# Message layers of a GNN kernel: rows in DRAM in node order, far table stored by blocks, one-byte destination lists

## The reference, cut to what matters

```python
def message_part(x, edge_index, ...):           # two layers
    h = x @ W_enc.T + b_enc
    row, col = edge_index
    for l in range(2):
        m = jnp.concatenate([h[row], h[col]], axis=-1)
        m = jax.nn.relu(m @ msg_W1[l].T + msg_b1[l])
        m = m @ msg_W2[l].T + msg_b2[l]
        agg = jax.ops.segment_sum(m, col, num_segments=N)
        upd = jnp.concatenate([h, agg], axis=-1) @ upd_W[l].T + upd_b[l]
        h = layer_norm(h + upd, ln_g[l], ln_b[l])
    return h @ W_out.T + b_out

def linear_part(x, edge_index, ...):            # three layers
    for i in range(3):
        agg = segment_sum(h[src], dst) / max(degree, 1)
        h = agg @ Wl[i].T + bl[i] + h @ Wr[i].T  # relu between layers
```

## Time and profile before

| | us |
|---|---|
| median of 3 runs | 3507.04 (3503.56 to 3512.03) |
| the profiled execution, its own time | 3502.89 |
| its span in the profile | 3501.0 |
| PE / DVE / ACT / POOL busy | 2972.4 / 2400.5 / 2058.7 / 800.4 |
| granted TensorE clock, mean | 0.931 of full speed |

### The profile page before, as it was taken

The page is one execution under the profiler, slowest core; times in us unless marked ns, Lnnn a source line. Parts: engine busy times, 40 slices in busy tenths (PEclk is TensorE's granted clock), DMA queues, the critical chain, the costliest instruction groups (busy, mean ns, idle before and its releaser), DMA issues.

```text
span 3501.0 us, 221482 instructions
## 1 busy us (share of the span) xinstructions
PE 2972.4 (85%) x88750; PEld 2729.9 (78%) x88750; DVE 2400.5 (69%) x5707; ACT 2058.7 (59%) x3873; POOL 800.4 (23%) x1161
## 2 busy tenths in 40 slices
PE   3665666699989998799989997789999799999998
PEld 2544544588878887688878887688888799999998
DVE  6899998555545556666645555699999865556555
ACT  1333333577766666777756665667777555555555
POOL 1222215200012225400012124334333411111111
PEclk7777777899999999999999999799999999999999
DMA  3000002699978883599977875055555478877888
GB/s 68 9 7 7 6 6 53 141 214 216 216 180 201 198 201 88 121 219 217 223 180 195 199 197 123 16 164 172 170 170 171 137 219 276 274 243 232 263 269 251
DMA packets 423266, 570.13 MB, mean 163 GB/s; under 512 B 129597, under 2 KB 277877, under 8 KB 423186
## 3 DMA queue, kind: packets, MB, share of 16 engines
q1 hardware_dynamic: 390475, 541.83, 57.2%
q0 software_dynamic: 8000, 16.40, 4.7%
q10 hardware_dynamic: 24710, 10.93, 1.2%
HBM read 459.97 MB, written 108.98 MB: 163 GB/s over the span
## 4 chain that ended last, share of the span: by engine, by line
PE 57%; DVE 16%; issue 9%; DMA 9%; SPq 3%; POOL 2%; ACT 2%; DVEq 1%; POOLq 0%; ACTq 0%
PE psum L1544 16%; PE psum L1315 15%; PE psum L1333 7%; PE psum L1319 7%; DMA tabf<-slots_turned 5%; DVE arena L1583 5%; PE psum L1531 4%; PE psum L1511 2%; PE psum L684 1%; PE psum L1519 1%; POOL arena L2019 1%; DVE Hf L1057 1%; DVE Hf L918 1%; DVE AGGf L963 1%; POOL tabf L2002 1%
## 5 line engine op out<-in xcount | busy, mean ns | idle before, releaser
L1315 PE MATMUL psum<-tabf,arena 125*32 125x128 f16 x40256 | 1112.4, 220 | 105.9 <-issue 58.4
L1315 PEld LDWEIGHTS psum<-tabf,arena 125*32 125x32 f16 x40256 | 949.5, 97 | 197.8 <-issue 129.9
L1319 PE MATMUL psum<-arena 96*32 96x128 f16 x20928 | 1054.3, 221 | 10.4 <-issue 10.4
L1366 ACT ACTIVATE arena<-psum 128x512 f32<-128x512 f32 x1300 | 770.5, 596 | 426.1 <-PE psum L1319 387.7
L1319 PEld LDWEIGHTS psum<-arena 96*32 96x32 f16 x20928 | 693.6, 95 | 19.0 <-issue 9.6
L1544 PE MATMUL psum<-tabr,cellr 125*125 125x256 f32 x5000 | 620.2, 284 | 14.4 <-ACT cellr L1462 14.4
L1544 PEld LDWEIGHTS psum<-tabr,cellr 125*125 125x125 f32 x5000 | 602.8, 187 | 15.8 <-issue 15.8
L1333 PE MATMUL psum<-arena 128*32 128x129 f32 x10400 | 564.1, 278 | 1.7 <-issue 1.7
L1462 ACT CAST cellr<-arena 125x630 fp32r<-125x630 f16 x500 | 359.9, 720 | 270.2 <-PE psum L1544 197.0
L1573 ACT CAST arena<-psum 125x500 f16<-125x500 f32 x625 | 358.9, 578 | 153.0 <-PE psum L1511 109.6
L1401 DVE TENSOR_TENSOR AGGf<-AGGf,psum 125x129 f32 x404 | 116.0, 287 | 435.6 <-PE psum L1333 432.9
(11 more groups left out here) (302 smaller groups left out, 4369.1 us busy)
## 6 DMA issues: line engine op xcount, KB each, us to landing
arena<-cells_kept SPq DMA_DIRECT2D x500, 315.0 KB
cells_kept<-arena SPq DMA_DIRECT2D x625, 126.0 KB
arena<-slots_turned SPq DMA_DIRECT2D x152, 384.0 KB
tabf<-slots_turned SPq DMA_DIRECT2D x150, 384.0 KB
arena<-slots_turned SPq DMA_DIRECT2D x152, 192.0 KB
tabf<-slots_turned SPq DMA_DIRECT2D x150, 192.0 KB
arena<-slots_turned SPq DMA_DIRECT2D x50, 512.0 KB
tabf<-slots_turned SPq DMA_DIRECT2D x50, 512.0 KB
```

The costliest lines, as they stand in the source:

```text
L1315: pe.matmul(psCell[b][q:q + GW, g * D:(g + 1) * D], fr, rows, start=g == 0 and p == 0, stop=False, tile_position=(0, q), skip_group_check= ...
L1319: m = pe.matmul(psCell[b][q:q + GW, g * D:(g + 1) * D], toB[part][:, here + q:here + q + GW], cur[:, part, g, :], start=g == 0 and 4 * k + ...
L1366: act.activation(msgs[:, SLOT[pos], :, 0:D], psCell[SLOT[pos]].rearrange("p (c d) -> p c d", d=D), ACT.Relu).then_inc(f_msg, 1)
```

## The change

Three things in the message layers, and what they need elsewhere:

- **Rows in node order.** `stack_dram` becomes [tile, 128, 256]: one row of 512 bytes per node with both parts together. A block of 10 tiles is stored by one transfer of 125 partitions instead of four. The load of a tile's own rows now has 256 entries of 256 bytes, in another order of the 64 rows (node, part) for which `row32` is computed anew.
- **Far table by blocks.** The source half goes to `table_dram[0]` by one transfer of 125 partitions per block of 10 tiles, right behind the block's store of destination rows. `rows_of_pair` and its 25 transfers of the first phase are gone.
- **One-byte destination lists.** The lists lie in two DRAM tensors, the source lists as f16 as before, the destination lists as uint8. The sort's store on ACT becomes three copies and two transfers; L1385's comparison reads uint8 and writes f16.

```diff
-        slots_dram = nc.dram_tensor("slots_turned", [NT + 2, 2, KS, RG * CELL], F16, kind="Internal").ap()
+        slots_dram = [nc.dram_tensor(f"slots_turned_{n}", [NT + 2, KS, RG * CELL], dt, kind="Internal").ap() for n, dt in (("from", F16), ("to", U8))]
-        stack_dram = nc.dram_tensor("rows_stacked", [NT, CP, GW, RG, D], F16, kind="Internal").ap()
+        stack_dram = nc.dram_tensor("rows_stacked", [NT, RG * GW, CROW], F16, kind="Internal").ap()
...
-                act.copy(STb[:, v], psTurn[0:TURNED, 0:CELL].bitcast(BF16).rearrange("p (u e) -> p u e", u=2))
+                turned = psTurn[:, 0:CELL].bitcast(BF16).rearrange("p (u e) -> p u e", u=2)
+                act.copy(STb[:, v], turned[0:TURNED])
+                act.copy(STu[TURN_TO:TURN_TO + TURNED, v], turned[TURN_TO:TURN_TO + TURNED])
                 act.copy(XT[:, tiles, :], psTurn[:, 256:512].rearrange("k (w p) -> k w p", w=2)[:, :, 0:P]).then_inc(o_ST, 1)
                 act.wait_ge(o_ST, m + 1)
-                act.dma_start(slots_dram[at].rearrange("o a k (g e) -> (a k g) o e", g=RG), STb[:, v]).then_inc(o_store[v], 16)
+                act.dma_start(slots_dram[0][at].rearrange("o k (g e) -> (k g) o e", g=RG), STb[:, v]).then_inc(o_store[v], 16)
+                act.dma_start(slots_dram[1][at].rearrange("o k (g e) -> (k g) o e", g=RG), STu[TURN_TO:TURN_TO + TURNED, v]).then_inc(o_store[v], 16)
...
-                sp.dma_start(stack_in[w].rearrange("q g d -> q (g d)"), stack_dram[at].rearrange("o p i g d -> (o p i) (g d)")).then_inc(f_stk[w], 16)
+                sp.dma_start(stack_in[w], stack_dram[at].rearrange("o (g i) (c d) -> (o i c) g d", g=RG, c=CP)).then_inc(f_stk[w], 16)
...
-                for g in range(RG):
-                    n = min(GW, P - g * GW)
-                    sp.dma_start(stack_dram[c * TB:(c + 1) * TB, :, 0:n, g, :].rearrange("t p i d -> i (t p) d"),
-                                 TABH[g * GW:g * GW + n, 1, c * TB:(c + 1) * TB].rearrange("i t p d -> i (t p) d")).then_inc(f_stack[c // 2], 16)
+                sp.dma_start(stack_dram[c * TB:(c + 1) * TB, 0:P].rearrange("t q e -> q t e"),
+                             TABH[:, 1, c * TB:(c + 1) * TB].rearrange("q t c d -> q t (c d)")).then_inc(f_stack[c // 2], 16)
+                sp.dma_start(table_dram[0].rearrange("(t p) d -> p t d", p=P)[:, c * TB:(c + 1) * TB, :],
+                             TABH[:, 0, c * TB:(c + 1) * TB].rearrange("p t c d -> p t (c d)")).then_inc(f_table, 16)
...
-                    if h == 0:
-                        rows_of_pair(bass.ds(i * 2, 2))
...
-            hold(pool, "pool", f_table, 16 * PAIRED * (l + 1))
+            hold(pool, "pool", f_table, 16 * NB_LOOPS * (l + 1))
...
-                    dve.tensor_scalar(toB[half][0:CP * GW, span], slist[v][half][0:CP * GW, 1, span], row32[:], None, ALU.is_equal).then_inc(f_toN, 1)
+                    dve.tensor_scalar(toB[half][0:CP * GW, span], slist[v][half][1][:, span], row32[:], None, ALU.is_equal).then_inc(f_toN, 1)
```

More of the change, by code:

```diff
@@ L17 @@
 I32 = mybir.dt.int32
+U8 = mybir.dt.uint8
 F32R = mybir.dt.float32r
@@ L79 @@
 KW = 14
-TURNED = 2 * KS * RG
+TURNED = KS * RG
+TURN_TO = 64
 FOLD = NT // 4 * 2
@@ L845, in sort_act @@
             m = SORTS - 1
-            store(m - 1, 1, slice(2 * m - 1, 2 * m + 1), slice(2 * m - 2, 2 * m), 16 * (SORTS // 2))
+            store(m - 1, 1, slice(2 * m - 1, 2 * m + 1), slice(2 * m - 2, 2 * m), 32 * (SORTS // 2))
             act.wait_ge(s_bound, 1)
@@ L1184, in lists @@
                 for a, rows in ((0, 128), (1, CP * GW)):
-                    sp.dma_start(slist[w][half][0:rows, a, 0:(k1 - k0) * RG * CELL], slots_dram[at, a, k0:k1, :]
+                    sp.dma_start(slist[w][half][a][0:rows, 0:(k1 - k0) * RG * CELL], slots_dram[a][at, k0:k1, :]
                                  .rearrange("o k e -> o (k e)").to_broadcast([rows, (k1 - k0) * RG * CELL])).then_inc(f_list[w][half], 16)
@@ L2414, in _ @@
             dve.wait_ge(s_const, 1)
-            for b in range(CP):
-                step.did(dve.tensor_scalar(row32[b * GW:(b + 1) * GW], row1[b * GW:(b + 1) * GW], float(b * GW), None, ALU.subtract))
+            step.did(dve.tensor_scalar(row32[:], row1[0:CP * GW], 0.5, -0.75, ALU.mult, ALU.add))
+            step.last()
+            step.did(dve.tensor_scalar(row32[:], row32[:], MAGIC, None, ALU.add))
+            step.last()
+            step.did(dve.tensor_scalar(row32[:], row32[:], MAGIC - 1.0, None, ALU.subtract))
             for g in range(RG):
```

42 lines of the change are left out of this document (19 added, 23 removed).

## The result

| | us |
|---|---|
| changed kernel, median of 20 runs | 3491.64 (3483.25 to 3501.73) |
| kernel before beside it, median of 20 | 3502.93 (3495.46 to 3512.21) |
| ratio, 95% interval | 0.9968 (0.9959 to 0.9976) |
| profiled execution of the changed kernel, its own time / span | 3485.43 / 3483.5 |
| PE / DVE / ACT / POOL busy | 2975.2 / 2568.7 / 2074.1 / 814.7 |

The change makes the kernel about 11 us faster, 0.3%. The forecast was 3504, no change; the measured median is 12 us under it and 0.4 us under the low end of the range. The profiled execution is one of the faster ones: its span is 17.5 us shorter than that of the kernel before, more than the medians differ.

A forecast was written before the change was run, and what follows sets the result against it. It took PE, and in the first layer partly late lists, to bound the first phases. First layer -1.6, second layer 0 and phase changes -1.5 summed to -3 us: 3504 us from 3507.04, range 3492 to 3530.

The forecast's parts named there:

- What bounds the kernel: First phases: PE and transfers nearly full; lists partly pace the first layer's (298.4 us), hardly the second's (291.4).
- the loop term: First layer's first phase: lists stop being late, 298.4 us becomes 289.9, a gain of 8.5 us.
- Second layer -1.5: Second layer's first phase: gains only 1.5 us, since DVE there mostly waits for PE.
- Why the lists were late: First-phase loop: 1.31 MB per tile falls to 1.05, 20% less, so the lists stop being late.
- Block stores: Layer starts: two 125-row stores on five engines, 12 us a block; +7.7 us first layer, +1.5 second.
- Sort: ACT: one more copy and issue, 25 times; hidden behind PE's wait for DVE, 18 us if uncovered.
- One-byte comparison: DVE's comparison at L1385: 606 ns grows by 0.5 us, about 1.0 estimated from the skill; hidden.
- the rival of one element a step: DVE becomes the bound: byte comparison takes 1.1 us more, +23 us on the forecast, 3527; chance 0.12.
- Second phases and phase changes: Second phases wait on PE, change nothing; stalls on issue where phases change shrink by 1.5 us in all, a guess.
- Queued block stores: Rival, SP's queue between tile 1's and tile 2's lists: 14.9 us a block or more, 3528; chance 0.22.
- The relief reaches further: Rival, second phases: a fifth of PE's idle time comes from late transfers, 9 us more gain, 3493; chance 0.16.
- The range: 3492 to 3530 us, leaving out about 2 in 10 on both sides; block prices of 10.8 and 14.9 us give 3496 and 3528.

The follow-up runs named there:

- e3: Changed kernel with the far table stored pair by pair in the first-phase loop again, not by blocks; ratio 0.9925 to the kernel before, chip B.
- e13: Changed kernel with each one-byte destination list loaded a second time, to all 128 partitions, into spare room; one run, 3506.37 us.
- e14: Kernel before with each pair-by-pair table store of 125 rows cut into 112 and 13 rows; ratio 0.9954 to the kernel before.
- e9: Changed kernel, unchanged, timed again as base for other kernels on chip D; ratio 0.9972 to the kernel before.
- e10: Changed kernel with two-byte destination lists, on chip D; ratio 1.0001 to the kernel before.
- e16: Changed kernel with the table stored in the loop, two-byte destination lists and all 125-row stores cut into 112 and 13; ratio 0.9954 to the kernel before.
- e1: Kernel before with only the far table moved from the loop to block stores; ratio 1.0102 to the kernel before, chip B.
- e2: Changed kernel with two-byte destination lists, on chip B; ratio 0.9948 to the kernel before.
- e4: Changed kernel with each block store of 125 rows cut into 112 and 13 rows; ratio 0.9920 to the kernel before, chip B.

## Why the prediction was wrong, step by step

- **What bounds the kernel: half right.** Lists late in the first layer, and their waits passing to PE, were read rightly. The step that failed is the floor of the loop term: "the first layer's first phase is thus paced in part by the lists; the second layer's hardly", so I gave the first layer what the second already had. The second layer's 291.4 us was no floor. It held long gaps at the loop's jump in the one trace and late lists in the other; freed of both, the phase took 277.7 us. This one term was -8.5 for -17.8. The chain of rows 5 had said how much the lists paced: from 585 to 1020 us, 42.3% of it is "DMA tabf<-slots_turned" and 6.0% "DMA arena<-slots_turned".
- **Second layer -1.5: mis-sized.** It was -13.7 in the first pair of traces, and -4 to -14 over the changed kernel's four. The waits for lists there, 15.2 us, were treated as slack because DVE mostly waited for PE; 67.1 us at L1401 said that PE was late, not why. PE's idle time of 8.85 us of 240 was there to be explained, and the waits on "issue" in that stretch were not among the rows I read.
- **Why the lists were late: half right.** I argued from total bytes, 20% less. Fewer bytes alone do repair the loop (e3), but the bytes were not too many for the 16 engines: more of them ran at full pace (e13, e14). What made the lists late in the first layer was the pair stores on five engines (e14). I had the rule and its trace for it (125 rows, five engines, rows 7), and used it for the block stores alone, not for `rows_of_pair`, which has the same 125 rows. The change both removed these stores and cut the bytes, and either is enough, so the lists stopped being late as forecast. It was luck that the part I had in mind was enough by itself. The DMA share after came out at 0.64, not 0.8.
- **Block stores: right.** 12 us a block taken, 12.0 measured; the first layer's start +7.5 from this for +7.7. Tile 2's list at 673.6 for a forecast of 671. In the second layer it came 2.1 us later for +1.5.
- **Sort: hidden, not quite.** The first comparison of the layer starts at 630.9 to 631.6 with the old sort (four traces) and at 629.6 to 635.6, mean 632.9, with the new one (15 traces): about 1.6 us by the means, not 0, and far from the 18 us of an uncovered copy. No run had the new sort's store alone.
- **One-byte comparison: right.** 1.0 us for 1536 elements, hidden in the first phases:

```profile
L1383 DVE TENSOR_SCALAR arena<-arena,row 64x1536 f16<-64x1536 uint8 x42 | 42.2, 1006 | 0.0
```

  It is 1006 ns for 606, and 1272 ns for 2048 elements (e9), so 512 elements take 266 ns and the rival of one element a step is out. The Trainium skill (VectorE: DVE Perf Modes, section on what auto-detection checks) has two elements a cycle here; the trace agrees, about 1.0 us as estimated. What it does to the second phases is on POOL, below: 0 to 0.05 us per tile on chip D.
- **Second phases and phase changes.** Taken at 0 and -1.5. The second phases were no zero: +3.6 and -1.1 us in the first two traces, but by the means of the changed kernel's four and the other's two S1 is 7.67 for 7.57 and S2 7.73 for 7.64, 9 to 10 us in all. Only e10's 2.4 us of it are tied to the lists' width; most goes with the node-order rows (e16 and e14, above), and why is open. By the same means the two first phases gain 28 us; this loss and the 12 us at the two starts take most of it back.
- **The rivals.** Queued block stores did not come: a store overlaps on its engines as the 29-row store did. "The relief reaches further" gave nearly the measured time, 3493, by another route: it had the second phases gain, and they lost; the first phases gained. That its number fits is luck.
- **The range** had no case in which the second layer's first phase was itself held back. Its low end came from the price of a block alone.

## What to carry to other kernels

A mean DMA share below 1 doesn't say that every engine has room: list which transfers in a loop use few of the 16 engines, and try them cut so that they use all. Cutting 125 rows into 112 and 13 cost SP one more issue and did more here (16 us in the loop of the kernel before, 20 us at the start of the changed one) than moving the transfer elsewhere, which made the kernel before 1% slower (e1). And before a stage of the same kernel is taken as the floor for another, its own idle time has to be explained from the waits, "issue" among them; a second trace of the same kernel showed that this floor was made of different things each time.

## What the runs showed of the hardware

- **A load and a store of 512-byte rows.** On five engines a load ran at 86 GB/s and the store at 109; on 16 the store ran at 199 and more.
- **Lists at 254 GB/s.** In 700 to 940 us the transfers, nearly all of them broadcast loads of lists, went from 184 to 254 GB/s with PE busy throughout (e13), while e1 was held at 207 GB/s and a share of 1.05 in its second layer with no store in the loop. So this share is no measure of what is left, and the rate that goes with a share of 1.01 to 1.05 varied from 207 to 231 GB/s (e1, e14, e16). Why e1 stayed late is open.
- **DVE's comparison and POOL's indirect load.** Issuing the overflow rows took POOL 970 ns before and takes 1210 ns with the one-byte comparison beside it, 1.27 us long for 0.74; here the changed kernel, 1000 to 1300 us:

```profile
L1275 POOL DMA_INDIRECT arena<-table_a,ovcur x40 | 48.4, 1210 | 31.4 <-POOL ovcur L1273 31.4
```

  The Trainium skill (SBUF — State Buffer, its warning that DVE blocks such a DMA) has the two share one pair of ports, held for a whole instruction; the trace agrees in direction, 0.24 us more on POOL for 0.53 us more on DVE. On chip D it cost at most 0.05 us per tile (e10 against e9). On chip B it may cost more: e2, with two-byte lists, has 6.84 and 6.88 us per tile in the second phases, e3 and e4 with one-byte lists 6.98 to 7.07, and PE's weight loads wait 8.2 us for the overflow rows in e2 and 15.0 and 17.3 in e3 and e4 (1000 to 1280 us). But e1, also with two-byte lists, has 7.02 and 6.93 and a wait of 15.7, so this isn't settled.
- **One of the chips.** On chip B the kernel before takes 3445 us for 3503 to 3507 elsewhere. The second phases are at 6.8 to 7.1 us per tile there and at 7.5 to 7.8 on the others, where PE stands about 0.5 us once per tile on "issue" in the second phases; on chip B it does so in none of the stretches read. Neither was expected, and nothing here explains it.
